# Weighted one-hots of the group stage: one comparison and one multiplication of 512 columns in place of four 128-column pointer instructions

## The reference, cut to what matters

```
xn  = layernorm(x)
gnn = segment_sum(edge_weight[:, None] * (xn @ W)[dst], src, 12500)
x   = x + gnn + mix(xn)      # linear attention with 8 heads, two layernorms, a small MLP
x   = x + ffn(layernorm(x))  # an MLP of 1024 hidden units for 6249 of the nodes, those of highest router score
```

## Time and profile before

| | |
|---|---|
| runs of the kernel before | 4204.99 to 4209.67 us, median 4208.03 |
| span of the profiled execution, first to last instruction | 4863.7 us |
| TensorE matmul, busy in the span | 3569.5 us (73%) |
| VectorE | 2693.1 us (55%) |
| GpSimd | 2549.3 us (52%) |
| ScalarE | 1493.0 us (31%) |
| first and last start of L1329, the one-hots of the group stage | 3312.4 and 4154.6 us |
| DMA traffic in the group stage (3320 to 4140) | 226.63 MB, 276 GB/s |

### The profile page before, as it was taken

One profiled execution on the slowest core, in us unless ns is written; L12 is line 12 of the kernel. 1 busy time (PEld: TensorE's weight loads), 2 busy tenths in 40 slices (PEclk: granted clock), 3 DMA queues, 4 the chain that ended last, 5 costly groups with the idle time before them and its releaser, 6 DMA issues. The chain is left out here.

```text
span 4863.7 us, 81669 instructions
## 1 busy us (share of the span) xinstructions
PE 3569.5 (73%) x15079; PEld 2574.4 (53%) x15079; DVE 2693.1 (55%) x9932; ACT 1493.0 (31%) x3369; POOL 2549.3 (52%) x2800
## 2 busy tenths in 40 slices
PE   5773777777777777777877777758999999101998
PEld 3551445555555555555555555536777777101887
DVE  6993333333333345555555555537999999853111
ACT  2220222333333234443444444412333333300322
POOL 0002655566655555555555555566777777136222
PEclk8886888888988887888888888878999999655999
DMA  5447333333333333333333333327898888124111
GB/s 169 166 143 258 122 117 117 117 121 123 120 118 117 117 126 120 126 119 116 128 120 123 124 120 124 116 102 231 277 276 278 276 275 278 57 73 149 54 54 43
DMA packets 432617, 706.73 MB, mean 145 GB/s; under 512 B 55659, under 2 KB 249194, under 8 KB 432427
## 3 DMA queue, kind: packets, MB, share of 16 engines
q1 hardware_dynamic: 336399, 443.02, 29.8%
q0 software_dynamic: 92736, 257.08, 14.8%
q10 hardware_dynamic: 3456, 6.34, 0.4%
HBM read 374.87 MB, written 333.92 MB: 146 GB/s over the span
## 5 line engine op out<-in xcount | busy, mean ns | idle before, releaser
L497 POOL DMA_INDIRECT sorted_rows<-rowbuf,posu x1664 | 1650.2, 992 | 1184.1 <-issue 1036.8
L675 PE MATMUL ps<-win,oht 128*128 128x256 f32 x3328 | 932.3, 427 | 206.0 <-ACT rowbuf L903 105.3
L903 ACT ACTIVATE rowbuf<-ps 128x512 f32<-128x512 f32 x832 | 483.8, 600 | 1499.7 <-remote 846.3
L675 PEld LDWEIGHTS ps<-win,oht 128*128 128x128 f32 x3328 | 698.9, 216 | 385.9 <-issue 144.4
L797 PE MATMUL ps<-rowbuf,oht 128*128 128x256 f32 x3520 | 829.5, 392 | 31.0 <-DVE oht L1329 24.5
L1329 DVE TENSOR_SCALAR oht<-cols,rowbuf 128x128 f32<-128x128 f32 x1760 | 810.8, 531 | 49.5 <-DMA rowbuf<-sorted_rows 38.1
L522 POOL TENSOR_TENSOR acc<-acc,node 128x256 f32 x880 | 659.3, 749 | 197.0 <-POOL acc L522 157.9
L797 PEld LDWEIGHTS ps<-rowbuf,oht 128*128 128x128 f32 x3520 | 610.0, 189 | 250.5 <-DVE oht L1329 175.4
L1181 DVE CUSTOM_DVE_ANT_0 scr<-ps,ohb 128x98 f32<-128x98 f32 x1664 | 331.0, 255 | 557.4 <-remote 433.4
L1163 DVE TENSOR_SCALAR oht<-ps,lane 128x512 f32<-128x512 f32 x216 | 162.0, 750 | 721.8 <-remote 415.4
L981 ACT ACTIVATE node<-ps 128x512 f32<-128x512 f32 x440 | 262.7, 597 | 597.8 <-PE ps L797 487.2
(11 more groups left out here) (240 smaller groups left out, 4656.1 us busy)
## 6 DMA issues: line engine op xcount, KB each, us to landing
rowbuf<-sorted_rows SPq DMA_DIRECT2D x440, 516.0 KB, 4.4
win<-support_rows SPq DMA_DIRECT2D x416, 128.0 KB
sorted_rows<-rowbuf,posu POOLq DMA_INDIRECT x1762
xn_rows<-acc SPq DMA_DIRECT2D x14, 896.0 KB, 4.5
xn_transposed<-acc SPq DMA_DIRECT2D x14, 896.0 KB, 4.2
support_rows<-acc SPq DMA_DIRECT2D x14, 896.0 KB, 5.2
acc<-xn_transposed SPq DMA_DIRECT2D x98, 128.0 KB
q_transposed<-acc SPq DMA_DIRECT2D x49, 256.0 KB
```

Source lines behind the costliest of these rows:

```text
L497: g.indirect_dma_start(rows_d, bass.IndirectOffsetOnAxis(posu[:, s:s + 1], 0), rowbuf[:, s, :], None).then_inc(scat[k], 16)
L675: last = mm(ps[:, MSG + h, t * C:(t + 1) * C], oht[:, k % 2, (2 * h + t) * P:(2 * h + t + 1) * P], win[:, k, :], start=True, stop=True)
L903: A(rowbuf[:, s:s + 2, 0:C], ps[:, MSG + h, :].rearrange("p (t c) -> p t c", t=2), ACT.Copy).then_inc(row_ready, 1)
```

## The change

The four `tensor_scalar` of a round become two `tensor_tensor` over all four tiles at once, with the same result. The first compares `cols`, repeated four times along the columns, with the nodes' places, each spread over 128 columns. The second multiplies the result in place with the weights, spread likewise. It reads what the first wrote, so VectorE waits for the first to finish (the new semaphore `ohe_ready`). The semaphore `ohw_ready` is counted up once a round and no longer four times, and TensorE waits for it once, ahead of the first matmul of a round. The other engines' instructions are the same.

```
-        sums_ready = sem("sums_ready")
+        sums_ready, ohe_ready = sem("sums_ready"), sem("ohe_ready")
...
                 for k in range(KB):
                     pe.wait_ge(r_in[k], 16 * (i + 1))
                     pe.wait_ge(sums_ready, KB * i + k + 1)
+                    pe.wait_ge(ohw_ready, KB * i + k + 1)
                     for h in range(2):
-                        grp = RG * i + 2 * k + h
                         for t in range(2):
-                            pe.wait_ge(ohw_ready, 2 * grp + t + 1)
                             s = 2 * h + t
...
                 for k in range(KB):
                     dve.wait_ge(r_in[k], 16 * (i + 1))
                     dve.wait_ge(grp_mm, RG * i + 2 * k + 6)
-                    for s in range(BT):
-                        r = BT * k + s
-                        v.tensor_scalar(oht[:, k % 2, s * P:(s + 1) * P], cols[:, :], rowbuf[:, r, C + 1:C + 2],
-                                        rowbuf[:, r, C:C + 1], ALU.is_equal, ALU.mult).then_inc(ohw_ready, 1)
+                    r = slice(BT * k, BT * (k + 1))
+                    o = oht[:, k % 2, :].rearrange("p (s e) -> p s e", s=BT)
+                    v.tensor_tensor(o, cols[:, :].unsqueeze(1).to_broadcast([P, BT, P]),
+                                    rowbuf[:, r, C + 1:C + 2].to_broadcast([P, BT, P]),
+                                    ALU.is_equal).then_inc(ohe_ready, 1)
+                    dve.wait_ge(ohe_ready, KB * i + k + 1)
+                    v.tensor_tensor(o, o, rowbuf[:, r, C:C + 1].to_broadcast([P, BT, P]),
+                                    ALU.mult).then_inc(ohw_ready, 1)
```

## The result

The changed kernel takes 4362.74 us (median of 4 runs, 4359.92 to 4364.40) against 4208.35 of before (4204.99 to 4209.67): 154.4 us slower, ratio 1.037, 95% interval 1.0355 to 1.0384.

What follows compares the result with a forecast made beforehand. VectorE and GpSimd excluding each other was taken as the bound: two turns of 0.55 + 0.585 make 2.26 us, plus 0.06 is 2.32 against 1.914; over 440 rounds +179, so 4208 + 179 = 4387 us, 8-in-10 range 4240 to 4510.

Steps and rivals of the forecast that it cites:

- case A: Group stage: VectorE and GpSimd exclude each other, preparations overlapped; round 2.32 us, +179, 4387 us; chance 0.61.
- turns of 0.55 + 0.585: Group stage: VectorE's 0.55 us after release plus GpSimd's 0.585 hold, two a round, 2.26 us.
- Case C: Group stage: VectorE and GpSimd exclude each other for whole durations, preparation included; round 2.83 us, +403, 4611; chance 0.06.
- the 0.06: Group stage: late rows and missed turns, 1.914 against 1.85 us before, kept in the new round, making 2.32.
- TensorE's wait for all four tiles costs nothing: Group stage: first matmul starts later but the round doesn't grow; TensorE has 1.73 us of work in 2.32.
- the loads' lead: Row loads in the group stage: 4.4 us to land, with 3 rounds of lead, 5.7 us, then 7.0.
- D: Group stage: two-input form doesn't collide with GpSimd; round 1.78 us, -59, 4149; chance 0.11.
- E: Group stage: exclusion plus TensorE's clock at 1.2 GHz 30% of the time; round 2.57 us, +291, 4499; chance 0.06.
- B: Group stage: part exclusion, 0.14 us less held per addition; round 2.05 us, +60, 4268; chance 0.13.
- The bound of before: Group stage before: VectorE and GpSimd exclude each other; two additions 0.92 apart make 1.85 of 1.914 us.
- The DMA share: DMA engines in the group stage: busy share to fall from 0.89 to about 0.73.

Runs made afterwards that it cites:

- e1: Changed kernel with each of GpSimd's 880 additions cut from 256 columns to 1; 4956.65 us beside 4881.57 for before, ratio 1.0131.
- p2: Changed kernel with one input of both new instructions in PSUM; 4290.15 us beside 4219.89 for before, ratio 1.0164.
- e6: Changed kernel with each load of rows halved to the first of the round's two groups; 5033.25 us beside 4880.62 for before, ratio 1.0327.
- e4: Kernel before with only TensorE's waits changed, one a round in place of four; 4996.69 us beside 4881.57 for before, ratio 1.0204.
- e5: As e1, with each load of rows halved; 4840.83 us beside 4880.62 for before, ratio 0.9925.
- e2: Kernel before with each of GpSimd's additions cut to 1 column; 4845.68 us beside 4881.57 for before, ratio 0.9918.
- p1: Kernel before with the columns' numbers read from PSUM, copied there once ahead of the stage; 4864.30 us beside 4880.62 for before, ratio 0.9975.

## Why the prediction was right, point by point

**The mechanism (case A) was right.** Forecast: a new instruction ends 0.55 us after the addition it stands behind; measured 0.546 to 0.552. Forecast: turns of 0.55 + 0.585 = 1.135; additions follow each other at 1.134. e1 and p2 show it from either side: it goes with the additions' columns, and with the second SBUF input. The Trainium skill's rule for two SBUF inputs (SBUF — State Buffer, section Who interferes with whom) holds for the new instruction, with one refinement that its words don't have: preparation overlaps. I wrote that the earlier trace rows agree with it for the old instruction; they show one engine standing still behind the other, but the old instruction has only one SBUF stream and is no case of that rule. Case C took the words literally and is refuted, 2.27 against its 2.83.

**The size was off by one term.** I added to the 2.26 us of two turns the 0.06 by which the old round exceeded its own 1.85. That was wrong: the changed round is 2.269, so the excess is 0.01. Late rows and missed turns are slack that the longer turn swallows: e6 shows it for the rows, and only 7 of 880 instructions started outside an addition, where the old ones missed 50 of 880 turns. 440 x 0.05 = 22 us is nearly the whole difference between 4387 and 4363.

**"TensorE's wait for all four tiles costs nothing" was wrong, and covered.** I looked at the halves of `oht` alone and at TensorE's busy time, 1.73 in 2.32, and did not follow a row buffer round its stations. I took the loads' lead for 3 rounds, 5.7 us before and 7.0 after. By the table it was 4.68 before (4.44 + 0.24, the load and the wait for VectorE) and 4.51 after, as a load is asked for only when TensorE has ended its round. The wait alone costs 106 us in the stage (e4). In the changed kernel it cost nothing visible only because the exclusion costs more (e6: halved loads win nothing; and over the stage VectorE stood idle before L1328 only 4.3 us for TensorE). The changed kernel with a finer wait was not run. The total came out right with one step unsound, and that was luck: an exclusion that cost less than about 0.15 us a round would have left the missed wait to set the time (e1, 2.07 against 1.91).

**The rivals.** D, no collision, forecast 4149, 59 faster. Had there been no collision, the changed kernel would still have been slower than before: e1, +75, and p2, +70 us. D had the wrong sign because of the same missed wait; and the 1.73 it gives TensorE is 1.81 in practice (e5, TensorE busy 200.00 of 200): there the step into a round and the step from its first record to the second take 0.26 each instead of 0.216, and 6 x 0.216 + 2 x 0.26 = 1.81. E, a falling clock, is refuted by the granted 1.00, the same from 2660 to 3660. B, a partial hold, is refuted by the 0.546.

**The bound of before.** The view that two engines' interplay made the 1.91 us is borne out only in part. With the additions cut (e2) or the exclusion removed (p1) VectorE's round falls from 1.90 to 1.12 and 1.37, and the round only to 1.85: TensorE and the loads stand right behind, 0.07 us away.

**The DMA share** was forecast to fall to 0.73, and is 0.80. I had scaled the share with the round (0.89 x 1.914 / 2.27 = 0.75); why it fell less than the traffic did stays open.

## What to carry to other kernels

Before merging small VectorE instructions into larger ones, count their SBUF inputs and look whether GpSimd reads SBUF at the same time: an instruction with two such inputs and a GpSimd instruction take turns, each in its full streaming length, and one input from PSUM ends that. The old form, with one SBUF stream at two columns in a column time, took turns too; there the stream from PSUM costs 0.06 us for 128 columns. When a semaphore is coarsened from tiles to rounds, add up the steps that each buffer must go through, load included and waits left out, and divide by the number of buffers; a busy share below one proves no slack. When two costs bound the same loop, remove each alone and both: here the difference to before was the larger one, not the sum, and a step can be free only because another is worse.

## What the runs showed of the hardware that was not expected

- An excluded instruction finishes its preparation while it stands still: it ends 81 to 89 ns after the addition's end for 128 columns at two per column time (0.49 ns each, see p1), 546 to 552 ns for 512 columns at 1.03, out of 332 and 691 ns alone. In both cases that is the streaming, 66 and 528 ns, and some 20 more; so only the streaming counts in a turn.
- The old `tensor_scalar`, with one SBUF stream and two SBUF pointer scalars, is excluded as well (up to 0.907 us), and the same instruction with its stream from PSUM is not (at most 0.414): there the pointer scalars and the output in SBUF don't collide.
- A load of 516 KB takes 4.0 to 4.6 us in the mean to land, with 1.8 to 2.5 in flight (load by round); one of 258 KB takes 2.63 us, with 1.2 to 1.5 in flight.
